# A vision-tower layer on one core: skip scales as 4-row products turned back, decay sums in rows of 512, new steady lists

## The reference, cut to what matters

```python
def _hydra(u, in_w, conv_w, conv_b, dt_bias, A_log, D, fcD_w, norm_w, out_w):
    zxbcdt = u @ in_w.T
...
    xBC = jax.nn.silu(_causal_conv(xBC, conv_w, conv_b))
    xs = xBC[..., :DIN]                      # DIN = 256
...
    y_fw = _ssm_scan(x4, dt_fw, A, Bm, Cm).reshape(b, l, DIN)
...
    y = y + xs * jnp.repeat(xs @ fcD_w.T + D, HD, axis=-1)   # the skip scales: NH = 4 heads
    yz = y * jax.nn.silu(z)
    y = yz * jax.lax.rsqrt(jnp.mean(jnp.square(yz), -1, keepdims=True) + 1e-05) * norm_w
    return y @ out_w.T
```

## Time and profile before

| | |
|---|---|
| timed runs, median | 2145.37 us |
| profiled execution | 2142.9 us |
| its span, first to last instruction | 2141.2 us |
| instructions | 53461 |

### The profile page before, as it was taken

The page is one execution under the profiler, slowest core; times in us unless marked ns, Lnnn a source line. Parts: engine busy times, 40 slices in busy tenths (PEclk is TensorE's granted clock), DMA queues, the critical chain, the costliest instruction groups (busy, mean ns, idle before and its releaser), DMA issues.

```text
span 2141.2 us, 53461 instructions
## 1 busy us (share of the span) xinstructions
PE 2070.2 (97%) x14483; PEld 1872.0 (87%) x14483; DVE 1767.5 (83%) x5080; ACT 1502.6 (70%) x3068; POOL 980.0 (46%) x1349
## 2 busy tenths in 40 slices
PE   3889999999999999999999999999999999999998
PEld 3767889999999999999999999999999999998988
DVE  6778988888888888888888888888888888887775
ACT  4777777677767777777777776777677777776652
POOL 3465644454445444454445444544454444543431
PEclk9999999999999999999999999999999999999999
DMA  4211312221122112221222122211221122212211
GB/s 127 80 60 37 91 37 68 69 69 50 54 69 69 54 49 69 69 69 34 69 69 69 37 66 69 69 51 53 69 69 55 48 69 69 69 35 68 75 43 36
DMA packets 90192, 132.65 MB, mean 62 GB/s; under 512 B 20507, under 2 KB 63687, under 8 KB 90134
## 3 DMA queue, kind: packets, MB, share of 16 engines
q1 hardware_dynamic: 89414, 129.33, 20.2%
q10 hardware_dynamic: 720, 2.62, 0.3%
HBM read 55.03 MB, written 76.74 MB: 62 GB/s over the span
## 4 chain that ended last, share of the span: by engine, by line
PE 54%; issue 21%; POOL 6%; DVE 3%; ACT 3%; POOLq 1%; DVEq 0%; ACTq 0%
PE bank L1901 19%; PE bank L2008 5%; PE bXYZ L2082 3%; PE bXYZ L2066 3%; POOL CB L923 2%; PE bank L1996 2%; PE bank L1962 2%; PE bXYZ L2094 2%; PE bank L1934 2%; ACT L1091 2%; POOL XD L874 1%; PE bXYZ L2042 1%; PE bXYZ L2113 1%; PE bXYZ L2024 1%; PE bank L1936 1%
## 5 line engine op out<-in xcount | busy, mean ns | idle before, releaser
L1901 PE MATMUL bank<-w_hi,XHI 128*128 128x392 f32 (+1 forms) x1560 | 597.6, 383 | 1.4 <-DVE XLO L1592 1.4
L1901 PE MATMUL bank<-w_lo,XHI 128*128 128x392 f32 (+1 forms) x1560 | 527.9, 338 | 0.0
L1901 PE MATMUL bank<-w_hi,XLO 128*128 128x392 f32 (+1 forms) x1560 | 527.5, 338 | 0.0
L1344 DVE SCALAR_TENSOR_TENSOR CX<-bXYZ,cw,CX 128x252 f32<-128x252 f32 (+5 forms) x804 | 344.9, 464 | 54.8 <-ACT CX L1029 54.7
L1901 PEld LDWEIGHTS bank<-w_hi,XHI 128*128 128x128 f32 x1560 | 294.4, 189 | 15.4 <-DVE XLO L1592 1.7
L1901 PEld LDWEIGHTS bank<-w_lo,XHI 128*128 128x128 f32 x1560 | 294.7, 189 | 8.9
L993 ACT ACTIVATE T<-bank 64x512 f32<-64x512 f32 x256 | 151.7, 592 | 208.7 <-PE bank L1996 204.1
L1901 PEld LDWEIGHTS bank<-w_hi,XLO 128*128 128x128 f32 x1560 | 293.1, 188 | 0.0
L923 POOL TENSOR_TENSOR CB<-CB,CM 128x126 f32<-128x126 f32 (+5 forms) x402 | 172.2, 428 | 190.3 <-ACT CM L993 161.6
L887 POOL TENSOR_TENSOR lone<-lone 128x1 f32<-128x1 f32 x65 | 35.4, 545 | 357.2 <-DVE lone L1536 357.0
L914 POOL TENSOR_TENSOR RB<-m_gt,AS 128x512 fp32r<-128x512 f32 x134 | 157.2, 1177 | 79.3 <-DVE AS L1610 79.3
(11 more groups left out here) (293 smaller groups left out, 5412.3 us busy)
## 6 DMA issues: line engine op xcount, KB each, us to landing
carried<-T SPq DMA_DIRECT2D x65, 512.0 KB, 4.5
T<-carried SPq DMA_DIRECT2D x65, 512.0 KB, 3.8
out<-HB SPq DMA_DIRECT2D x129, 256.0 KB, 3.2
tables<-tab SPq DMA_DIRECT2D x8, 560.0 KB, 4.8
TB<-tables SPq DMA_DIRECT2D x62, 70.0 KB, 2.7
carried<-U SPq DMA_DIRECT2D x65, 64.0 KB, 3.5
XM<-carried SPq DMA_DIRECT2D x65, 64.0 KB, 4.5
XI<-in_x SPq DMA_DIRECT2D x128, 32.0 KB, 2.7
```

What stands on the lines that cost most here:

```text
L1344: inc(STT(CX[:, c, :, s:CS], src[:, :, 0:CS - s], cw[:, c, k:k + 1], CX[:, c, :, s:CS], ALU.mult, ALU.add), "conv")
L1901: ins = mm(bank[:, 0:c1 - c0], xs_[:, 1 - p, k, :], ws[:, k, c0:c1], start=(c0 == C2 and k == 0 and n == 0), stop=(c0 == C2 and k == KC - ...
```

## The change

The skip scales take the stream as the moving operand: for each contraction half one product of `fcT` (4 columns, stationary) with 256 positions, both summed into 4 rows of the same bank. A new ScalarE call `keep_skip` copies these 4x256 numbers to SBUF (into rows of the scratch SQ), and a new TensorE call `turn_skip` ahead of `mix` brings them back to columns with two fp32 products against the identity. `skip_scale` waits for `turn_skip` (`fcs`) instead of `grams`. The decay sums are four products of 512 columns. The input's real part is written by `keep_x` straight into its place in W, the imaginary part into a fifth slot of W, so that XTC and GpSimd's copy `shift_none` go. All steady lists are reordered; the first and last lists get the two new calls.

```diff
-        XTC = sb("XTC", [P, 2, 2, CS])
-        W = sb("W", [P, 2, 4, CS])
+        W = sb("W", [P, 2, 5, CS])
+        XR, XJ = W[:, :, 0, :], W[:, :, 4, :]
...
-        FC0 = 2 * CS
+        FT, FC0 = slice(2 * CS, 2 * CS + 2 * P), 2 * CS + 2 * P
+        DT = SQ[0:NH, :]
...
-                    def shift_none():
-                        if A:
-                            wait(pool, i, xtc=1)
-                            wait(pool, i - 1, km=2)
-                            apart(pool)
-                            inc(pool.tensor_copy(W[:, :, 0, :], XTC[:, 0, :, :]), "wi")
...
+                    def keep_skip():
+                        if G:
+                            wait(act, r, gram=1, g4=2)
+                            copy(DT, bY[0:NH, FT], "fct")
...
                     def skip_scale():
                         if G:
-                            wait(dve, r, gram=1)
+                            wait(dve, r, fcs=1)
...
                             wait(pe, r, dtc=1, xs=5, conv=NCONV, sz=1)
-                            for a in range(2):
-                                for c in range(2):
-                                    mm(bY[:, FC0 + NH * a:FC0 + NH * (a + 1)],
-                                       CX[:, c, 2 * a:2 * a + 2, :].rearrange("p g t -> p (g t)"),
-                                       fcT[:, c, :], start=(c == 0), stop=(c == 1))
+                            for c in range(2):
+                                mm(bY[0:NH, FT], fcT[:, c, :], CX[:, c, :, :].rearrange("p g t -> p (g t)"),
+                                   start=(c == 0), stop=(c == 1))
...
+                    def turn_skip():
+
+                        if G:
+                            wait(pe, r, fct=1)
+                            for a in range(2):
+                                ins = mm(bY[:, FC0 + NH * a:FC0 + NH * (a + 1)], DT[:, P * a:P * (a + 1)],
+                                         ident[0:NH, 0:NH], start=True, stop=True)
+                            inc(ins, "fcs")
...
-                            for a in range(2):
-                                for n, (m, dec) in enumerate(((earlier, RF), (earlier, RF), (later, RB), (later, RB))):
-                                    ins = mm(bZ[:, 256 * a:256 * (a + 1)], m[:, :],
-                                             dec[:, n % 2, NH * a:NH * (a + 1), :].rearrange("p h t -> p (h t)"),
-                                             start=(n == 0), stop=(n == 3))
+                            for n, (m, dec) in enumerate(((earlier, RF), (earlier, RF), (later, RB), (later, RB))):
+                                ins = mm(bZ[:, :], m[:, :], dec[:, n % 2, :, :].rearrange("p h t -> p (h t)"),
+                                         start=(n == 0), stop=(n == 3))
```

The steady lists, where the prediction speaks of them. TensorE, start to the first half of S4D:

```diff
                         turn_xs()
+                        bases(0, 0, 1)
                         turn_x()
-                        bases(0, 0, 1)
                         route(0, 1)
-                        route(2, 3)
                         bases(1, 0, 1)
                         route(3, 4)
+                        route(2, 3)
+                        route(5, 6)
                         route(6, 7)
+                        turn_skip()
                         mix()
-                        route(5, 6)
                         s4d(0)
```

More of the change, by code:

```diff
@@ L788, in load_x @@
                 def load_x(t, p):
-                    wait(sp, t - 2, xt=1, xswap=1, v1=1, wr=1, v2=1, wi=2)
+                    wait(sp, t - 2, xt=1, xswap=1, v1=1, wr=1, v2=1, wi=1)
                     apart(sp)
@@ L976, in body @@
                         add_bc(2)
+                        deviation_1()
                         add_bc(3)
@@ L1078, in keep_x @@
                             wait(act, i, xt=1)
-                            wait(act, i - 1, wr=1, wi=2)
-                            copy(XTC[:, :, :, :].rearrange("p a b c -> p (a b c)"), bK[:, 0:256], "xtc")
+                            wait(act, i - 1, wr=1, wi=1, km=2)
+                            copy(W[:, :, 0:5:4, :].rearrange("p b a c -> p a b c"), bK[:, 0:256].rearrange("p (a b c) -> p a b c", a=2, b=2), "xtc")
                     def keep_xs():
@@ L1174, in body @@
                         weight_hi(1)
+                        keep_skip()
                         exp_decays()
@@ L1261, in body @@
                     else:
+                        keep_xs()
+                        exp_decays()
                         keep_x()
-                        exp_decays()
-                        keep_xs()
+                        keep_skip()
                         keep_h(0, 0)
@@ L1292, in body @@
                         norm_2()
+                        scale_bc(6)
+                        split_hi(0)
                         silu_x()
-                        split_hi(0)
                         silu_bc(0)
@@ L1402, in shift_real @@
                             wait(dve, i - 1, km=2)
-                            inc(TT(W[:, :, 1:4, :], XTC[:, 0, :, :].unsqueeze(2).broadcast_to([P, 2, 3, CS]),
+                            inc(TT(W[:, :, 1:4, :], XR.unsqueeze(2).broadcast_to([P, 2, 3, CS]),
                                    TB[:, p, :, TSR].unsqueeze(3).broadcast_to([P, 2, 3, CS]), ALU.mult), "wr")
@@ L1839, in body @@
                         softplus(8)
+                        softplus(9)
+                        softplus(10)
                         stats_2(3)
-                        softplus(9)
+                        softplus(11)
                         conv(5, 0)
-                        softplus(10)
+                        softplus(12)
+                        split_decays(0)
                         shift_2()
-                        softplus(11)
-                        softplus(12)
+                        split_decays(1)
                         weighted_lo()
-                        split_decays(0)
-                        split_decays(1)
                         conv(5, 1)
+                        decays_forth(0)
                         conv(6, 0)
@@ L1991, in s4d @@
                             if b == 0:
-                                wait(pe, i, xtc=1, wsum=1, wi=2, vsum=1)
+                                wait(pe, i, xtc=1, wsum=1, vsum=1)
                             else:
@@ L2234, in body @@
                         turn_xs()
+                        bases(0, 0, 1)
                         turn_x()
-                        bases(0, 0, 1)
                         route(0, 1)
-                        route(2, 3)
                         bases(1, 0, 1)
                         route(3, 4)
+                        route(2, 3)
+                        route(5, 6)
                         route(6, 7)
+                        turn_skip()
                         mix()
-                        route(5, 6)
                         s4d(0)
+                        bases(0, 1, 2)
                         route(1, 2)
-                        bases(0, 1, 2)
                         project_x()
+                        bases(0, 3, 4)
                         route(4, 5)
+                        s4d(1)
                         route(7, 8)
-                        s4d(1)
-                        bases(0, 3, 4)
                         turn_y()
+                        bases(0, 2, 3)
                         bases(0, 4, 5)
-                        bases(0, 2, 3)
                         project_out()
@@ L2261, in body @@
                         up(1)
+                        bases(1, 2, 3)
+                        bases(1, 3, 4)
+                        turn_a(0)
+                        bases(0, 6, 7)
+                        bases(1, 7, 8)
+                        turn_a(1)
+                        bases(1, 5, 6)
+                        turn_h()
+                        bases(1, 6, 7)
                         bases(1, 4, 5)
-                        bases(1, 5, 6)
-                        turn_a(0)
-                        bases(1, 2, 3)
                         bases(0, 5, 6)
-                        bases(0, 6, 7)
-                        turn_a(1)
-                        turn_h()
-                        bases(1, 7, 8)
-                        bases(1, 3, 4)
-                        bases(1, 6, 7)
                         lora(0)
                         lora(1)
-                        lora(2)
                         turn_d(0)
                         down()
+                        lora(2)
                         turn_d(1)
```

56 lines of the change are left out of this document (25 added, 31 removed).

## The result

The changed kernel takes 2210.14 us (median of 4, 2209.86 to 2210.19), the kernel before 2145.08 us (2142.43 to 2146.96): ratio 1.030, 95% interval 1.029 to 1.031. It is slower by 65 us. The forecast was 2177 us, in a range from 2128 to 2198: the sign was right, the size half.

A forecast was written before the change was run, and what follows sets the result against it. TensorE was taken as the bound: a step costs its matmuls plus under 0.6 us of waits. +0.06 + 0.54 - 0.02 = +0.58 us, with 0.10 recovered, gave +0.48 x 67 = +32 us: 2177 us, range 2128 to 2198.

The forecast's parts named there:

- What bounds the kernel: Whole steady step of 30.38 us: TensorE's matmuls set its time, plus less than 0.6 us of waits.
- What a record costs: TensorE fp32 records: 0.112 us with 4 moving columns, 0.215 with 256; a tile change about 0.09.
- row form: Skip scales on TensorE: four 256-column records plus two tile changes, 1.04 us against 0.98 removed, +0.06 a step.
- turn: `turn_skip` ahead of `mix` on TensorE: four records of 0.112 us plus a tile change, +0.54 us a step.
- decay sums: TensorE's eight fp32r records of 256 columns become four of 512, 0.23 us each: -0.02 us a step.
- Other engines: GpSimd loses a 0.75 us copy, ScalarE gains 0.4 us, VectorE's `skip_scale` gets a new wait for `turn_skip`.
- cover of 0.3 us for `s4d(0)`: Behind `mix`: `shift_sum` ends near 1024.0, `s4d(0)` is due near 1024.3, so it need not wait.
- Sum: Steady step: +0.58 us of records, 0.10 of 0.59 us of waits recovered, net +0.48 x 67 = +32 us.
- the overlap of two passes: Rival: two passes of one product overlap in a narrow tile; 2120 to 2133 us, middle 2127; chance 24%.
- The product doesn't go to a narrow tile: Rival on the row form: no tile changes there, +0.43 us a step, about 2168 us; no separate chance given.
- The lists take back nearly all the waits: Rival on the steady lists: 0.55 us of waits regained, +0.03 us a step, 2147 us; chance 10%.
- The moved chain becomes the wait: Rival: later `keep_x` chain against earlier `s4d(0)`, 0.4 us more in 54 steady steps, 2199 us; chance 10%.

The follow-up runs named there:

- e3: The changed kernel's new arithmetic with the steady lists of the kernel before, plus the two new calls: 2175.1 us, ratio 1.0145 to the kernel before.
- e4: The kernel before with the new steady lists, without the two new calls, `shift_none` kept: 2182.5 us, ratio 1.0177 to the kernel before.
- e12: e3 with the row form split into two column tiles and two copies: 2162.8 us, ratio 1.0076 to the kernel before.
- e1: The changed kernel with ScalarE's `keep_y` put back ahead of `keep_h(1,1)`: 2214.6 us, ratio 1.0326 to the kernel before.
- e11: e3 with the two products of `turn_skip` as transposes: 2154.1 us, ratio 1.0041 to the kernel before.

## Why the prediction was wrong

- *What bounds the kernel* was half right. "A step costs what its matmuls cost, plus less than 0.6 us of waits" holds for the lists that it was read from. That VectorE and ScalarE have only 6% of the chain says that they are not the limit in that order of calls; it says nothing of another order. Their share is 11% in e3, under the old lists, but 18% in e4 and 22% in after, under the new ones. And the earlier trace rows had a sign: `lora` waited for VectorE's `HWS` in 16 of 34 steps, so that in these the chain to `HWS` had no slack left.
- *What a record costs*, *row form*, *turn*, *decay sums*: right, each to 0.01 us. The trace has 0.95 and a tile change ahead of it (about 0.1 in e3) for 1.04, 0.53 for 0.54, and decay records 0.23 apart. e3 is the new arithmetic alone: 30 us. Its steady step is 0.42 longer; against 0.58 of records that leaves 0.16 of waits that went. The entry of `s4d(0)` (L1996 in the earlier trace rows, 0.11 a step) is not among e3's and makes up most of it. 54 x 0.42 + 13 x 0.58, the 13 steps with other lists, is 30.2.
- *Other engines*: the wait of `skip_scale` came and cost nothing by itself. The cover of 0.3 us for `s4d(0)` held; no wait stands there.
- *Sum*: here is the step that failed: "Of the 0.59 us of waits I take 0.10 as recovered". Under old lists 0.16 is recovered; the new lists then cost 0.71 a step (31.46 less 30.75), 35 us in all. It also put the recovery at the wrong call: the wait of `turn_y`, which was to go, stayed (3.5 us in 16 waits in after, 3.6 before). I had asked of some moved calls on TensorE whether their input was ready, and followed ScalarE only as far as `keep_skip`. I did not follow two swaps on other engines that the change makes: `keep_h(1,1)` ahead of `keep_y`, 0.6 us ahead of `project_out`'s input, and on VectorE `gated_b` behind `layer_out` and behind statistics that had filled its wait. And "that of `lora` (L1934) follows `turn_h` by three blocks as before" looked at the distance on TensorE, where the releaser in the earlier trace rows is VectorE's `HWS`, which stands behind `GT` in VectorE's list.
- *Rivals*: the overlap of two passes fell (starts 0.215 apart in one tile); what runs side by side is two tiles (e12). "The product doesn't go to a narrow tile" fell by the tile change in the trace (0.31 instead of 0.215 behind the last record); its +0.43 comes to +0.40 by its own terms, and nothing rests on it. "The lists take back nearly all the waits" had the wrong sign. "The moved chain becomes the wait" was the right kind, at the wrong place (`s4d(0)`) and for 22 us instead of 35, and the range, which went up to 2198 with it, allowed for only one new wait.

The sign came out right by the half that was priced right, the records; the 35 us of the lists were not foreseen.

Still open: which calls in VectorE's order behind `GT` hold the 11 us, and which in TensorE's and GpSimd's lists the 6.

## What to carry to other kernels

When a diff rewrites the order of several engines' queues, price the order as a change of its own: for each swap on any engine ask which engine's next input is behind it, and follow that to the end of the step; run the order with the old arithmetic, as e4 did, to see its price alone. A wait that moves to a later call when one call is put back (e1) points at a chain over several engines; here the calls that had to be put right together were found by comparing the same stretch in several traces, not by the largest wait. And try an fp32 product that only turns data as a transpose: here it cost 0.21 us instead of 0.53.

## What was not expected of the hardware

- A transpose of 4 partitions by 128 columns costs less than half of the plain fp32 product with the same operands' shapes: two transposes, one record each, take 0.21 us to the next line (e11), two products, two records each, 0.53. I had taken the price of the product.
- Two tiles of 32 columns that read the same 128 partitions run side by side: in e12 8 records start in pairs 0.006 to 0.009 us apart, pairs 0.11 apart, so that 128 columns cost half of what they cost in one tile (0.215 for 256). Padding one stationary from 4 to 32 columns changed next to nothing there (0.55 against 0.54).
